# Two routed expert layers around attention: another order of the first eight tiles, loaded by ScalarE as soon as the tile table is there

## The reference

```
x = L0_attn_x                                # 8 x 256 x 256: 2048 tokens of 256
x = x + 0.5 * ffn(layernorm(x))
x = x + attention(layernorm(x))              # 16 heads of 16
x = x + 0.5 * ffn(layernorm(x))

ffn(x): t = rmsnorm(x) * norm_w
        logits = t @ gate_w.T + gate_b       # 16 experts
        vals, idx = top_k(logits, 4); gates = softmax(vals)
        h = t @ w1[e].T + b1[e]              # 512 columns
        y = (min(h_even, 7) * sigmoid(1.702 * ..) * (clip(h_odd) + 1)) @ w2[e].T + b2[e]
        return x + sum over the 4 chosen experts of gate * y
```

## Time and profile before

| | |
|---|---|
| median of 3 runs | 817.67 us (814.58 to 818.37) |
| the profiled execution, its own time | 817.23 us |
| its span, first to last instruction | 815.5 us |
| TensorE busy | 685.8 us (84%) |
| VectorE busy | 607.9 us (75%) |
| ScalarE busy | 431.0 us (53%) |
| GpSimd busy | 457.3 us (56%) |
| transfers | 188.85 MB, mean 232 GB/s |

### The profile page before, as it was taken

The page is one execution under the profiler, slowest core; times in us unless marked ns, Lnnn a source line. Parts: engine busy times, 40 slices in busy tenths (PEclk is TensorE's granted clock), DMA queues, the critical chain, the costliest instruction groups (busy, mean ns, idle before and its releaser), DMA issues.

```text
span 815.5 us, 17266 instructions
## 1 busy us (share of the span) xinstructions
PE 685.8 (84%) x4640; PEld 541.3 (66%) x4640; DVE 607.9 (75%) x1443; ACT 431.0 (53%) x920; POOL 457.3 (56%) x446
## 2 busy tenths in 40 slices
PE   1877639999999998359999999885699999999970
PEld 1544327788888887347777777553478888888860
DVE  4876819777777776546778888867887777777777
ACT  3566325555555555326677666655245555555550
POOL 6877734666666667442235523347446666666670
PEclk9999999999999999688999999996699999999995
DMA  7999978868888762354445334146766788885864
GB/s 298 347 399 377 366 243 330 306 206 288 270 300 276 254 214 99 110 208 155 155 156 190 121 134 155 53 180 232 241 216 221 244 270 268 269 269 162 301 208 175
DMA packets 87418, 188.85 MB, mean 232 GB/s; under 512 B 13072, under 2 KB 37920, under 8 KB 85792
## 3 DMA queue, kind: packets, MB, share of 16 engines
q1 hardware_dynamic: 47104, 106.07, 38.2%
q10 hardware_dynamic: 26448, 41.92, 15.4%
q0 software_dynamic: 13776, 39.75, 12.9%
HBM read 105.46 MB, written 65.45 MB: 210 GB/s over the span
## 4 chain that ended last, share of the span: by engine, by line
PE 40%; DVE 10%; issue 3%; POOL 3%; DMA 1%; ACT 1%; ACTq 0%; DVEq 0%; POOLq 0%
PE s_psT L936 12%; PE s_psG L960 6%; PE s_psS L1455 3%; DVE s_a_nm L1712 3%; PE s_psO L1490 3%; PE s_psG L1427 3%; PE s_psS L917 2%; PE s_psS L903 2%; POOL rows L1348 2%; DVE all_x L2158 2%; PE s_psT L1471 1%; PE s_psT L1475 1%; PE s_psG L1440 1%; PE s_psG L1537 1%; DMA rows<-s_a_row,s_a_slot_i 1%
## 5 line engine op out<-in xcount | busy, mean ns | idle before, releaser
L1123 POOL DMA_INDIRECT kbuf<-s_e_own_ys,s_e_own_place x79 | 80.7, 1021 | 66.9 <-ACT s_e_own_ys L1069 59.9
L1123 POOL DMA_INDIRECT kbuf<-f_e_ys,f_e_place x79 | 80.1, 1014 | 67.0 <-ACT f_e_ys L1069 59.8
L936 PE MATMUL f_bank<-f_e_w,f_e_th 128*128 x316 | 114.5, 463 | 1.9 <-ACT f_e_th L1091 1.9
L936 PE MATMUL s_psT<-s_e_own_w,s_e_own_th 128*128 x316 | 113.4, 460 | 1.8 <-ACT s_e_own_th L1091 1.8
L1348 POOL DMA_INDIRECT rows<-s_a_row,s_a_slot_i x64 | 62.6, 978 | 78.8 <-DVE s_a_slot_i L1840 61.8
L1712 DVE TENSOR_REDUCE s_a_nm<-s_psS 128x4 f32<-128x1024 f32 x64 | 78.2, 1223 | 30.0 <-PE s_psS L1455 29.6
L999 DVE TENSOR_TENSOR s_e_own_hb<-s_psT,s_e_own_bias 128x512 f32<-128x512 f32 x79 | 54.5, 690 | 40.2 <-PE s_psT L936 40.2
L999 DVE TENSOR_TENSOR f_e_hb<-f_bank,f_e_bias 128x512 f32<-128x512 f32 x79 | 54.5, 690 | 39.5 <-PE f_bank L936 38.6
L1979 ACT ACTIVATE s_a_pT<-s_psT 128x1024 f32<-128x1024 f32 x62 | 63.3, 1021 | 33.4 <-PE s_psT L1475 33.4
L596 POOL DMA_INDIRECT rows<-f_r_row,f_r_slot_i x64 | 66.9, 1046 | 23.0 <-issue 18.5
L936 PEld LDWEIGHTS f_bank<-f_e_w,f_e_th 128*128 128x128 f32 x316 | 60.6, 192 | 22.3 <-issue 3.5
(11 more groups left out here) (360 smaller groups left out, 1825.3 us busy)
## 6 DMA issues: line engine op xcount, KB each, us to landing
w_split<-stage ACTq DMA_DIRECT2D x10, 1536.0 KB, 8.3
f_e_w<-w_split SPq DMA_DIRECT2D x24, 512.0 KB, 6.4
s_e_own_w<-w_split SPq DMA_DIRECT2D x24, 512.0 KB, 4.6
f_e_tb<-rows ACTq DMA_DIRECT2D x80, 144.0 KB, 4.2
s_e_tb<-rows ACTq DMA_DIRECT2D x80, 144.0 KB, 2.9
stage<-w_raw SPq DMA_DIRECT2D x11, 768.0 KB, 8.8
s_a_qs<-s_a_qk SPq DMA_DIRECT2D x32, 256.0 KB, 2.5
s_a_ks<-s_a_qk SPq DMA_DIRECT2D x30, 256.0 KB, 2.5
```

Of the source, the lines that this page charges most:

```text
L936: last = pe.matmul(psH[j][:, :], left[:, p % 2, j, k * P:(k + 1) * P], w1[:, bass.ds(buf, 1), h, k * I2:(k + 1) * I2], start=n == 0, stop= ...
L1123: pool.indirect_dma_start(out=kbuf[:, :], out_offset=bass.IndirectOffsetOnAxis(ap=place[:, n:n + 1], axis=0), in_=ys[:, n, :], in_offset=N ...
```

## The change

- The order of tiles: tiles 0 and 1 of each of experts 0 to 3 come first, then what is left of these four, then the others. `tile_columns` works with 20 segments (`NSEG`) instead of 16: `size` holds tiles of a segment, `ahead` what is subtracted for each segment passed, `step_s` the step of the expert number.
- `EARLY` is 8: eight tiles are loaded when their own groups have landed. Each loads its `need` into a register by itself.
- `begin` (wait for the table, block of offsets, `fetch(0)`, `fetch(1)`) stands on ScalarE ahead of `kept(7)` in the first layer and ahead of `routed_gates(7)` in the second. `AHEADP` is 3, and step -1 fetches pair 2 only.
- The pads of experts 12 to 15 move from ScalarE's start into its steps 0 to 3, behind the step's fetch, with a semaphore of their own that fetches 6 and 7 wait for. The padding counted by `padded` is that of experts 0 to 7.
- Splitting, first layer: SyncE stores expert 11 ahead of its pads; the low part of 12 comes behind the table and the counts; 13 moves into steps 0 and 1, 14 to steps 1 to 3. Second layer: the low parts of 1, 2 and 3 come in steps -1, 0 and 1, and the counts in step 4.

```diff
-NEED, EARLY = 3 * NT + 2 * NE + TOP * RINGS, 4
+NEED, EARLY = 3 * NT + 2 * NE + TOP * RINGS, 8
+FIRST_E, FIRST_N = 4, 2
+NSEG = NE + FIRST_E
...
-    one.link(one.engine.tensor_scalar(tiles["nt"][:, :], tiles["nt"][:, :], 1.0, None, ALU.max))
-    one.link(one.engine.tensor_tensor_scan(tiles["tend"][:, :], c["one_e"][:, :], tiles["nt"][:, :], 0.0, ALU.mult, ALU.add))
-    one.link(one.engine.tensor_tensor(tiles["tbeg"][:, :], tiles["tend"][:, :], tiles["nt"][:, :], ALU.subtract))
+    one.done(one.engine.tensor_scalar(size[:, F:NSEG], nt[:, :], 1.0, None, ALU.max))
+    one.done(one.engine.tensor_scalar(ahead[:, F:NSEG], nt[:, :], 1.0, None, ALU.max))
+    one.link(one.engine.tensor_scalar(tiles["spare"][:, :], nt[:, 0:F], 1.0, 1.0, ALU.max, ALU.subtract))
+    one.done(one.engine.tensor_tensor_scan(ahead[:, 0:F], c["one_s"][:, 0:F], tiles["spare"][:, :], float(FIRST_N), ALU.mult, ALU.min))
+    one.link(one.engine.tensor_tensor_scan(size[:, 0:F], c["one_s"][:, 0:F], tiles["spare"][:, :], float(FIRST_N), ALU.mult, ALU.min))
+    one.done(one.engine.tensor_tensor(ahead[:, F - 1:2 * F - 1], ahead[:, F - 1:2 * F - 1], size[:, 0:F], ALU.subtract))
+    one.link(one.engine.tensor_tensor(size[:, F:2 * F], size[:, F:2 * F], size[:, 0:F], ALU.subtract))
+    one.link(one.engine.tensor_tensor_scan(tiles["ends"][:, :], c["one_s"][:, :], size[:, :], 0.0, ALU.mult, ALU.add))
...
@@ route
+        split.store(sp, 11)
         sp.wait_ge(s_ends, 1)
         pad_rows(sp, m.phase, table, rows, c, s_pad, FIRST, some=range(NE - FIRST))
...
-        split.low(dve, BEHIND)
+        for e in in_cycle[NG - 1]:
+            split.low(dve, e)
...
-        act.wait_ge(s_ends, 1)
-        pad_rows(act, m.phase, table, rows, c, s_pad, FIRST, some=range(NE - FIRST, NE))
+        begin(act)
         kept(NG - 1)
-        split.high(act, BEHIND)
@@ experts
-    NBUF, NSEC, NY, RING, BANK, AHEADP = 4, 5, 8, 8, 8, 4
+    NBUF, NSEC, NY, RING, BANK, AHEADP = 4, 5, 8, 8, 8, 3
...
-            if s == -1 and not first_layer:
-                split.low(dve, NBUF - 1)
+            if not first_layer and s + 2 in range(1, NBUF):
+                split.low(dve, s + 2)
+            if not first_layer and s == NBUF:
+                routed.counts(dve)
...
+    def fetch(act, p):
+        at = rows_at[0]
+        if p % (BANK // 2) == 0:
+            at.load(p // (BANK // 2))
+        if p == EARLY // 2:
+            routed.rows(act)
+            routed.other_rows(act)
+        if p in (NE // 2 - 2, NE // 2 - 1):
+            routed.last_rows(act, p - AHEADP)
+        if p >= RING:
+            act.wait_ge(s_ys, 2 * (p - RING) + 2)
+        for j in range(2):
+            if 2 * p + j < EARLY:
+                need = act.alloc_register(f"{m.phase}_need{2 * p + j}")
+                act.load(need, table[0:1, NEED + 2 * p + j:NEED + 2 * p + j + 1])
+                act.wait_ge(routed.s_landed, act.snap(need, min_val=1, max_val=NG + 1))
+                carry(act, s_carrya)
+                act.free_register(need)
+            act.dma_start(tb[:, (2 * p + j) % (2 * RING), :], rows[bass.ds(at(2 * p + j), P), :]).then_inc(s_tb[p % RING], 16)
+
+    def begin(act):
+        routed.table(act)
+        rows_at.append(Column(act, "o", 0, NE * REGION))
+        fetch(act, 0)
+        fetch(act, 1)
...
-            for p in range(1 if s == -1 else s + AHEADP, s + AHEADP + 1):
-                if pair(p):
-                    fetch(p)
+            if pair(s + AHEADP):
+                fetch(act, s + AHEADP)
+            if 0 <= s < FIRST:
+                pad_rows(act, m.phase, table, rows, c, routed.s_pad, FIRST, some=range(NE - FIRST + s, NE - FIRST + s + 1))
@@ attention
         again.low(dve, 0)
-        again.low(dve, 1)
         routed_biases(b)
...
-        act.wait_ge(routed.s_ends, 1)
-        pad_rows(act, m.phase, table, rows, c, routed.s_pad, FIRST, some=range(NE - FIRST, NE))
         again.high(act, 2)
         again.high(act, 3)
+        begin(act)
         routed_gates(b)
```

102 lines of the change are left out of this document (48 added, 54 removed).

## The result

The changed kernel takes 854.62 us (median of 4 runs, 849.46 to 858.72); the kernel before beside it takes 818.02 (814.58 to 819.14). The ratio is 1.045, 95% interval 1.038 to 1.052: 37 us slower, where 13 were forecast, and above the top of the range, 842. The direction is right, the size is off by nearly three times.

What follows compares the result with a forecast made beforehand. The prediction took expert-stage steps to be bound by TensorE alone, so any wait there adds time. Its terms, -5.5 + 0.7 + 2 + 1 + 15 = +13.2 on 817.23 us, gave about 830 us, range 812 to 842.

Steps and rivals of the forecast that it cites:

- First start: Start of the first layer's expert stage: ScalarE issues tile loads earlier, first transposes at 108.5 against 113.99; -5.5 us (4 to 7 gained).
- More splitting in the steps: First layer's expert steps: splitting of experts 13 and 14 moved into them lengthens steps, partly hidden; +0.7 us (0 to 1.5).
- Pads and later weight loads: Pads in steps 0 to 3 and later weight loads for experts 4 to 6: hidden, counted as nothing.
- Second start: Start of the second layer's expert stage: begin ahead of routed_gates(7) delays bias matmuls and transposes; +2 us (0 to 4.5).
- VectorE's work: Second layer's steps: low parts of experts 1 to 3 and the counts moved in, partly fitting free time; +1 us (0 to 3).
- One pair less of lead: Steps of both expert stages: with AHEADP 3, tile loads beside weight loads come late and TensorE waits; +15 us (11 to 27).
- A: Rival on the expert steps: loads are in time or waits vanish in slack, so no change, 815.4 us; chance 0.22.
- B: Rival on both starts: ScalarE reaches the loads early, gaining 7 and 1 us, with loads in time, 809 us; chance 0.16.
- C: Rival: ScalarE's order at the second start costs the whole 4.5 us and the lead its full 27, 847 us; chance 0.04.
- D: Rival on the first start: the first load meets SyncE's longer queue, no gain, 835 us; chance 0.58 together with the forecast.

Runs made afterwards that it cites:

- a_lead4: The changed kernel with AHEADP back at 4 and nothing else taken back; ratio 1.0142 to the kernel before.
- a_old_order: The changed kernel with FIRST_N 0 for 2, so the tiles come in the order of before; ratio 1.0459 to the kernel before.
- b_lead3: The kernel before with AHEADP 3 for 4 and nothing else; ratio 1.0242 to the kernel before.
- a_again: The changed kernel itself run once more, without an edit; ratio 1.0446 to the kernel before.
- a_small_w: The changed kernel with only 16 columns of each weight part loaded from the fifth expert on; ratio 1.0102 to the kernel before.
- c_pads_13: The changed kernel taken back except begin ahead of kept(7) in the first layer and the new tile order with eight early loads; ratios 1.0115 and, run again, 1.0035.
- the c kernels: c_pads_13 and its variant with expert 13's parts left in the steps and the stores at steps 0 and 2; ratios 1.0115 and 1.0105 to the kernel before.

## Why the prediction was right and wrong

- **First start, -5.5**: measured -5.6, by the path that was told, but the number is partly luck: the pair's second load went out at 103.9 and not at 102.4, and landed in 4.4 us and not in 6.1. Not foreseen: that with the load early, ScalarE's path to the first `th` is next in line.
- **More splitting in the steps, +0.7 (0 to 1.5)**: together with pads and stores, measured +3.7 (first stage of a_lead4 against before, 201.7 to 198.0). Of that, expert 13's parts gave 1.2 when undone, inside the bounds; 14's were not undone. It was costed from the row of one kind of work, while pads, stores and a raw load are issued by ScalarE at the same place.
- **Pads and later weight loads, nothing**: the weight loads cost nothing that shows (a_old_order has them early and no shorter stage). The pads in the steps, put at nothing, weren't hidden: they are part of the 3.7, 1.6 us by the fifth step (8.9 to 7.3), and 1.8 together with the moved store (7.9 to 6.1).
- **Second start, +2 (0 to 4.5)**: measured +2.7 between the stages, and undone by moving `begin` (-2.8).
- **VectorE's work, +1 (0 to 3)**: measured +5.4 with all of it (second stage of a_lead4 against before), 3 to 4.5 of it shown by undoing. What failed here: free time of an engine, 1.2 us of a step, was deducted, as if the work could go into it. The counts stood in the chain between steps instead, and cost nearly all of their length in the changed kernel; for the low parts no timeline is shown.
- **One pair less of lead, +15 (11 to 27)**: the term that decides, as told, and the step of the prediction that failed: the mechanism is right and the size is not. Measured by a_lead4 26.2, by b_lead3 28.7, and 36.7 in a_again's execution. It has two parts. The waits are 19.9 us (24.4 in a_again, 18.6 in b_lead3), 5 above my choice. Scaling the late loads of the trace had given 27.5, some 25 loads late by 1.1 us each; 18 came, late by 1.1 us each. The allowance that a late load helps the next one took off 12.5 us where 7.6 would have been right, and whether it is the reason for the 7.6 no run shows. The second part was in no term: TensorE's own busy time is 6.5 us longer than in a_lead4.

In the profiled execution the change cost 32.2 us for the 13.2 forecast. Of the 19.0 too much, by the measurements above the lead has 11.2, VectorE's work 4.4, splitting, pads and stores 3.0, and the second start 0.7; 0.3 came back elsewhere. The terms' own upper bounds add up to 32 us, which is 849; the range ended at 842 all the same, so it left out what its own parts allowed. The median of the four runs is another 5 us above the profiled execution, the fastest of them; a_again shows that the first stage alone can take 10 us more.

The stall and what follows it, in the table of stretches of the changed kernel (the granted clock is the third value from the end) and its timeline:

```profile
243.00:245.00 2.00, 0.98 (x6) 0.84 (x7) 0.96 (x3) 0.63 (x1) 1.39 (x2) 1.00 0.60 204
245.00:247.00 2.00, 2.00 (x8) 1.46 (x7) 0.32 (x1) 0.60 (x1) 0.88 (x1) 0.51 0.87 310
247.00:249.00 2.00, 2.00 (x9) 1.49 (x9) 1.57 (x3) 0.13 (x1) 0.00 (x0) 0.64 0.39 47
249.00:251.00 2.00, 2.00 (x17) 1.88 (x16) 1.49 (x4) 1.14 (x3) 0.11 (x1) 1.00 0.87 285
```

```profile
244.02 0.33 PE L924 MATMUL f_bank<-all_ident,f_e_tb 128*128 128x128 f32 x1 [2.61 <-DMA f_e_tb<-rows]
...
245.29 1.20 PE L957 MATMUL f_bank<-f_e_w,f_e_tl 128*128 x2
...
248.58 0.70 PE L957 MATMUL f_bank<-f_e_w,f_e_tl 128*128 x2
```

TensorE waits 2.61 us, works on at 2.4 GHz, and is then granted 0.51, which is 1.2 GHz, for some 3.5 us: two matmuls take 1.20 us and, once the clock is back, 0.70. The step of the stall takes 8.5 us and the one behind it 6.8 for 5.1. So a stall of 2.6 us costs 5.1 (3.4 + 1.7). Waits and longer busy time together account for the term: in the first stage the waits of 10.1 and 5.0 us more of busy time than in a_lead4 (200.49 to 195.47) make 15.1, for 14.3 found; in the second 9.8 and 1.5 make 11.3, for 11.9; in a_again's first stage 15.0 + 9.7 = 24.7, for 24.2; in b_lead3's two stages against before 12.4 and 15.8, for 11.8 and 16.9.

The clock is only a part of the longer busy time. TensorE's busy time multiplied by what its granted clock lacked, summed over windows of 1 us, is 3.4 us in the first stage of the changed kernel. Half of it stands behind the stall above, and half behind a wait of 1.47 us at 131.46 that was for VectorE's `al` and not for a tile load:

```profile
132.00:134.00 2.00, 2.00 (x9) 1.56 (x8) 1.72 (x3) 0.66 (x2) 0.00 (x0) 0.60 0.86 280
```

a_lead4 has the same wait without a fall, and a_small_w has it with one. In the second stage the clock falls only in the first steps, in both kernels. In a_again the same sum is 8.1 of the 9.7 us, in b_lead3's two stages 1.7 of 3.5 and 4.6 of 6.1. So of the 11 us by which the term was too small, 5 are waits and 6 are longer busy time, of which the clock explains 3.4 at most in the changed kernel's own profile; the rest of it is not explained.

The Trainium skill's "TensorE: Matmul & The Clock Gate", section "HAM oscillation — how this bites in real kernels", warns that the clock falls again and again in kernels whose TensorE waits for DMAs. The trace agrees that falls follow such waits, here even behind single waits shorter than those the section describes, though not behind each. The prediction should have asked for it, having used the clock at the second start.

The rivals: A and B needed loads in time, and 18 waits show late ones. C named 847 by a costlier second start; the start was cheap (2.7), and the lead's 27 that it assumed was near the 26.2 measured, so its number is close for one of its two reasons. D didn't happen.

**Open.** On chip 2 the start of the changed kernels isn't earlier than that of b_lead3, which has the old start (125.7 in a_lead4, 124.4 in b_lead3). Their tables come at 119.4 and 116.5. The chain of small operations that makes the table is drawn out there. It has more operations in a_lead4, but c_pads_13, which has the same chain, had its table at 116.4. Two operations of it, in the changed kernel's profile and in that of a_lead4 on chip 2:

```profile
94.84 0.14 DVE L307 TENSOR_SCALAR f_r_col<-f_r_tn 128x1 f32<-128x1 f32 x1
95.02 0.16 DVE L308 TENSOR_TENSOR f_r_col<-f_r_col,f_r_past_all 128x1 f32<-128x1 f32 x1
```

```profile
106.13 0.14 DVE L307 TENSOR_SCALAR f_r_col<-f_r_tn 128x1 f32<-128x1 f32 x1
108.18 0.16 DVE L308 TENSOR_TENSOR f_r_col<-f_r_col,f_r_past_all 128x1 f32<-128x1 f32 x1 [1.91 <-DVE f_r_col L307]
```

Why isn't shown, and no profile of the kernel before exists from there; so the ratios of the c kernels on chip 2 (1.010 and 1.012, against 1.0035 for the same c_pads_13 on chip 3) are not explained, nor is what the changed kernel itself would take there.

## What to carry to other kernels

A prefetch distance is a number of microseconds between issue and use, to be held against the slowest landings beside other traffic, not the median; here 3 us of earlier issue in the same step were worth a whole pair of depth. Where TensorE is bound by its own work and starts to wait a little and often, leave room in the range for a lower clock and longer busy time behind the waits, and let the range reach as far as its own terms do. Free time of a helper engine is no room for work: look at where in its program the work stands, what the next step waits for behind it, and count each DMA issue as such work.

## What the runs showed of the hardware

TensorE's clock fell from 2.4 to 1.2 GHz inside a stage that had it busy for 200.5 of 216 us, behind single waits of 1.5 and 2.6 us (at 131.46 and 244.02 in the changed kernel) and, in a_again, of 2.2 us (at 188.24), and came back after 3 to 4 us. Behind another wait of 2.4 us (at 188.44 in the changed kernel) and behind all waits of up to 1.7 us in its second stage it did not fall, nor did it behind the same 1.5 us wait in a_lead4 (at 147.13). Behind its first steps no stage of the kernel before shows a fall. In a_again, which had a wait of 3.1 us up to 272.32, the clock had fallen before TensorE went on:

```profile
270.00:272.00 2.00, 0.00 (x0) 0.00 (x0) 0.06 (x1) 0.77 (x2) 1.81 (x3) 0.86 0.87 227
272.00:274.00 2.00, 1.68 (x6) 1.32 (x7) 0.00 (x0) 0.00 (x0) 0.77 (x1) 0.50 0.85 303
```

The kernel before takes 6 to 7% longer on chip 2. b_lead3, which has its program but for one constant, shows there 10 us more ahead of the first stage and 45 more between the stages than the kernel before elsewhere, while a step that TensorE fills takes 5.1 us on every chip.
